# Two state-space stages: their preparation moved into the stages before them, and every fourth unit's product given to GpSimd

## What is computed

```python
x = einsum('ed,bld->bel', in_proj_w, ctx)              # ctx (4, 256, 128), not the residual
u = silu(depthwise_conv4(x) + conv_b)
x_dbl = einsum('ke,bel->bkl', x_proj_w, u)             # 8 + 16 + 16 rows: dt_lo, Bm, Cm
delta = softplus(einsum('er,brl->bel', dt_proj_w, dt_lo) + dt_proj_b)
def step(state, xs):                                   # over the 256 tokens, 16 states a channel
    dA = exp(d_t[..., None] * A)
    state = state * dA + (d_t * u_t)[..., None] * B_t[:, None, :]
    y_t = einsum('ben,bn->be', state, C_t)
    ...
y = (ys + D[None, :, None] * u) * silu(z)              # z is the layernorm of the residual
```

## Time and profile before

| | |
|---|---|
| time, median of 3 runs | 1869.97 us (1865.51 to 1870.55) |
| the profiled execution, its own time | 1874.38 us |
| its span, first to last instruction | 1872.6 us |
| busy: PE, DVE, ACT, POOL | 60%, 59%, 25%, 32% of the span |
| mean granted clock of PE, share of 2.4 GHz | 0.806 |
| mean DMA rate | 99 GB/s |

### The profile page before, as it was taken

How to read it: one execution, slowest core, us unless ns; L and a number is a source line. 1 busy time by engine, 2 the same in 40 slices (tenths; PEclk the granted TensorE clock), 3 DMA queues, 4 the chain that set the end, 5 groups by cost and what they waited for, 6 DMA issues and landing times. The chain is left out here.

```text
span 1872.6 us, 21908 instructions
## 1 busy us (share of the span) xinstructions
PE 1121.4 (60%) x5649; PEld 707.2 (38%) x5650; DVE 1106.5 (59%) x1869; ACT 476.3 (25%) x883; POOL 604.8 (32%) x646
## 2 busy tenths in 40 slices
PE   5315556995085961552697802698847558846870
PEld 2201134774044730211454602576624124435750
DVE  5759974444354537998876695411448537562463
ACT  2143311221012533330211100333212226602320
POOL 0016623444631103661200073034232212214555
PEclk8669976998587975996798856799978559968995
DMA  6023347993307011421000001224410550078843
GB/s 217 1 93 135 134 127 232 304 310 92 98 23 113 4 58 59 157 90 67 0 1 1 1 11 34 75 99 130 125 42 12 68 57 4 3 230 269 254 134 101
DMA packets 135045, 185.54 MB, mean 99 GB/s; under 512 B 34656, under 2 KB 98802, under 8 KB 134332
## 3 DMA queue, kind: packets, MB, share of 16 engines
q1 hardware_dynamic: 99084, 131.89, 25.0%
q0 software_dynamic: 12608, 31.26, 6.0%
q10 hardware_dynamic: 23280, 21.50, 3.5%
HBM read 140.97 MB, written 30.74 MB: 92 GB/s over the span
## 5 line engine op out<-in xcount | busy, mean ns | idle before, releaser
L172 PE MATMUL psum<-w_ident,h 128*128 128x128 f32 x144 | 32.0, 414 | 145.8 <-DVE h L150 145.8
L1542 DVE TENSOR_REDUCE l3x_neg<-psum 128x2 f32<-128x512 f32 x128 | 81.0, 684 | 61.6 <-PE psum L1414 61.5
L462 PE MATMUL psum<-l0s_conv_out,w_ident 128*128 128x512 f32 x128 | 65.0, 632 | 83.5 <-DVE l0s_conv_out L559 83.5
L462 PE MATMUL psum<-l1s_conv_out,w_ident 128*128 128x512 f32 x128 | 65.5, 637 | 81.4 <-DVE l1s_conv_out L559 81.4
L160 POOL TENSOR_SCALAR rstd<-moments 128x4 f32<-128x4 f32 x24 | 6.5, 270 | 320.0 <-DVE moments L143 320.0
L1517 ACT ACTIVATE l3x_work<-psum 128x512 f32<-128x512 f32 x128 | 72.3, 599 | 89.6 <-PE psum L1436 89.3
L428 POOL TENSOR_TENSOR l0s_xpad<-l0s_du,l0s_bc 128x1024 f32<-128x1024 f32 x32 | 75.2, 2353 | 32.6 <-DVE psum L555 32.4
L428 POOL TENSOR_TENSOR l1s_xpad<-l1s_du,l1s_bc 128x1024 f32<-128x1024 f32 x32 | 75.2, 2353 | 32.5 <-DVE psum L555 32.4
L184 ACT ACTIVATE hT<-psum 128x512 f32<-128x512 f32 x40 | 21.7, 595 | 250.0 <-PE psum L172 210.1
L172 PEld LDWEIGHTS psum<-w_ident,h 128*128 128x128 f32 x144 | 28.0, 218 | 150.4 <-DVE h L150 139.6
L985 PE MATMUL psum<-l0f_w_in,l0f_xT 128*128 (+1 forms) x224 | 78.0, 472 | 3.3 <-ACT l0f_xT L1031 3.3
(11 more groups left out here) (643 smaller groups left out, 3179.5 us busy)
## 6 DMA issues: line engine op xcount, KB each, us to landing
l0f_w_in<-in_l0f_w_in SPq DMA_DIRECT2D x56, 352.0 KB, 8.3
l0s_bc<-l0s_scratch SPq DMA_DIRECT2D x16, 1024.0 KB, 5.2
l1s_bc<-l1s_scratch SPq DMA_DIRECT2D x16, 1024.0 KB, 5.3
l3f_w_in<-in_l3f_w_in SPq DMA_DIRECT2D x64, 192.0 KB, 4.1
...
```

The source lines that it names most:

```text
L172: ins = nc.tensor.transpose(m.psum[:, at:at + P], m.h[:, t, k * P:(k + 1) * P], m.ident[:])
L462: ins = nc.tensor.matmul(m.pair(2 + c)[:, cols], lhsT=m.ident[:], rhs=rhs[:, cols], start=start, stop=stop, skip_group_check=True)
L1542: ins = nc.vector.tensor_reduce(self.neg[k % 2][:, :, hl], bank[:, 0:self.keys].rearrange("p (q k) -> p q k", q=self.maxima), AX_X, ALU.ma ...
```

## The change

The function `state_space` becomes a class with methods that other stages call. Layer 0's preparation runs within stage 0, layer 1's at the end of stage 2, in buffers borrowed there; what is kept until the scan is `u`, `delta`, for layer 0 also the first slot of `bc`, and for layer 1 two chunks that lie in the space of the weights `l3x_` and `l3a_`, which are now loaded in stage 5 (by SP, behind that stage's own three loads). The scan stage itself loads the slots at its start, forms `du` on DVE, then the layernorm, and runs the units. In every fourth unit (`handed`: u % 4 == 3, always chunk 1) DVE scans into an SBUF tile `handed_state` and POOL multiplies it by C into `handed_read`; the waits count accordingly. `convolve`, `project_in`, `project_x`, `project_dt`, `take_in`, `take_conv`, `take_x`, `take_dt` and `store_rows` hold the same instructions as L538/L540, L439, L446, L453, L492, L496, L501, L505 to L513 and L393/L397 before; `soften` is L582 and `softplus_tail`. In stage 0 the two attention chunks get exp and relu tiles of their own.

```diff
@@ -273,22 +278,27 @@
...
+    e = [[m.sb(f"l0_exp{c}{i}", [P, T]) for i in range(2)] for c in range(KD)]
+    relu = [m.sb(f"l0_relu{c}", [P, 2, T]) for c in range(KD)]
+    r = [[relu[c][:, i, :] for i in range(2)] for c in range(KD)]
     sums = [m.sb(f"l0_sum{i}", [P, T]) for i in range(2)]
     att = m.sb("l0_att", [P, KD, T])
-    phi_in = m.sem("l0_phi_in")
     chunk_done = m.sem("l0_chunk_done")
+    flat = lambda x: x[:].rearrange("p t d -> p (t d)").rearrange("p (k t) -> p k t", k=KD)
+    ssm.prepare(xpad=m.sb("l0s_xpad", [P, KD, B, D_CONV - 1 + S])[:], conv=m.sb("l0s_conv_out", [P, KD, T])[:], t_sq=flat(m.h),
+                relu=relu[0][:], xdbl=m.hT[0:X_DBL, 0, :])
...
+            m.load_weights(sp, [g for g in reversed(m.w_loaded) if g not in FIRST_WEIGHTS + LATE_WEIGHTS])
+            ssm.store_rows(sp)
...
+            ssm.project_in(pe, (m.pair(2), m.pair(3)))
             norm_tensor(m, pe, n)
             m.wait_weights(pe, "l0_attn")
+            pe.wait_ge(ssm.x_out, KD)
             for c in range(KD):
                 for i, x in enumerate("qkv"):
                     project(m, pe, jobs, x + str(c), wcols(w, KD * i + c), feature_rhs(m.hT), KD,
                             turn=j if c + i == 0 else None)
+            pe.wait_ge(jobs.emptied["vector"], 1)
+            ssm.project_x(pe, m.pair(0, X_DBL))
+            pe.wait_ge(jobs.emptied["scalar"], 2 * KD)
+            ssm.project_dt(pe, (m.pair(1), m.pair(2)))
             pe.wait_ge(chunk_done, KD)
+            pe.wait_ge(ssm.dt_taken, KD)
...
+            ssm.take_in(act, (m.pair(2), m.pair(3)))
             norm_scalar(m, act, j)
             for c in range(KD):
                 for i, x in enumerate("qk"):
                     name = x + str(c)
                     jobs.wait_filled(act, name)
-                    if c:
-                        act.wait_ge(chunk_done, c)
-                    nc.scalar.activation(e[i][:], jobs.pair(name), ACT.Exp).then_inc(phi_in, 1)
-                    nc.scalar.activation(r[i][:], jobs.pair(name), ACT.Relu).then_inc(jobs.empty(name), 1)
+                    nc.scalar.activation(e[c][i][:], jobs.pair(name), ACT.Exp)
+                    nc.scalar.activation(r[c][i], jobs.pair(name), ACT.Relu).then_inc(jobs.empty(name), 1)
+            ssm.take_conv(act)
+            ssm.take_x(act, m.pair(0, X_DBL))
+            act.wait_ge(chunk_done, 1)
+            ssm.take_dt(act, (m.pair(1), m.pair(2)))
...
+                ssm.convolve(dve, c)
+            for c in range(KD):
                 dve.wait_ge(jobs.emptied["scalar"], 2 * c + 2)
...
                 nc.vector.tensor_tensor(att[:, c, :], sums[0][:], sums[1][:], ALU.mult).then_inc(chunk_done, 1)
+            ssm.soften(dve, 0)
             add_tokens(m, dve, jobs, ("out0", "out1"), scale=16 ** -0.5)
...
+            ssm.soften(dve, 1)
...
+    def soften(self, dve, c):
+        nc, o = self.m.nc, self.m.dve_order
+        dve.wait_ge(self.act_dt, c + 1)
+        e, q = self.delta[:, c, :], self.t_sq[:, c, :]
+        o.link(dve, nc.vector.tensor_tensor(e, e, q, ALU.mult))
+        softplus_tail(dve, nc.vector, o, e, q, self.conv[:, c, :], self.relu[:, c, :], e)
...
+        handed = lambda u: u % 4 == 3
+        reads = [sum(not handed(v) for v in range(u)) for u in range(UNITS + 1)]
+        by_pool = [sum(handed(v) for v in range(u)) for u in range(UNITS + 1)]
+        handed_state, handed_read = m.sb(g + "handed_state", [P, T]), m.sb(g + "handed_read", [P, T])
...
+                norm_gpsimd(m, pool, n)
+                pool.wait_ge(du_ready, 1)
+                def read_for(i, q0, u):
+                    pool.wait_ge(summed, q0 + (u + KD + 1 - 4))
+                    nc.gpsimd.tensor_tensor(handed_read[:], handed_state[:], bc[u // KD][:, 1, :], ALU.mult).then_inc(
+                        handed_ready, 1)
+                def group(i, q0, first):
+                    for s in range(SLOTS):
+                        pool.wait_ge(bc_in[s], (i + 1) * 16)
                         for c in range(KD):
...
+                            u = s * KD + c
+                            pool.wait_ge(scanned, q0 + u + 1)
+                            nc.gpsimd.tensor_tensor(drive[c], du[:, c, :], bc[s][:, 0, :],
+                                                    ALU.mult).then_inc(drive_ready, 1)
+                            if u >= KD and handed(u - KD):
+                                read_for(i, q0, u - KD)
+                            if not first and u < KD and handed(u - KD + UNITS):
+                                read_for(i, q0 - UNITS, u - KD + UNITS)
+                group(0, 0, True)
+                with pool.Fori(1, GROUPS) as i:
+                    group(i, i * UNITS, False)
+                pool.wait_ge(scanned, GROUPS * UNITS + KD)
+                read_for(GROUPS - 1, (GROUPS - 1) * UNITS, UNITS - 1)
...
+                            if handed(u):
+                                pe.wait_ge(handed_ready, i * by_pool[UNITS] + (by_pool[u] + 2))
+                            else:
+                                pe.wait_ge(read_ready, i * reads[UNITS] + (reads[u] + 1 + KD))
...
+                            if handed((unit - KD) % UNITS):
+                                act.wait_ge(scanned, i * UNITS + (unit + 1))
+                            else:
+                                before = reads[unit + 1 - KD] if unit >= KD else reads[unit + 1 - KD + UNITS] - reads[UNITS]
+                                act.wait_ge(read_ready, i * reads[UNITS] + (before + KD))
...
+                dve.sem_inc(handed_ready, 1)
+                for c in range(KD):
+                    o.mark(nc.vector.tensor_tensor(du[:, c, :], delta[:, c, :], u[:, c, :], ALU.mult))
+                o.wait(dve)
+                for c in range(KD):
+                    first = delta[:, c, :].rearrange("p (b s) -> p b s", s=S)[:, :, 0:1]
+                    o.mark(nc.vector.memset(first, 1e25))
+                o.wait(dve)
+                dve.sem_inc(du_ready, 1)
+                norm_vector(m, dve, n)
+                def unit(i, s, c):
+                    u, q = s * KD + c, i * UNITS + (s * KD + c)
+                    dve.wait_ge(decay_ready, q + 1)
+                    dve.wait_ge(drive_ready, q + 1)
+                    if handed(u):
+                        dve.wait_ge(handed_ready, i * by_pool[UNITS] + (by_pool[u] + 1))
+                    out = handed_state[:] if handed(u) else state[c]
+                    nc.vector.tensor_tensor_scan(out, decay[c], drive[c], 0.0, ALU.mult, ALU.add).then_inc(scanned, 1)
+                    if not handed(u):
+                        dve.wait_ge(scanned, q + 1 + KD)
+                        dve.wait_ge(summed, q + 1)
+                        nc.vector.tensor_tensor(read[c], state[c], bc[s][:, 1, :], ALU.mult).then_inc(read_ready, 1)
...
+SOFTENED = (0, 20, 32)
...
             by_steps(pe, groups, step, 3)
+            if ssm is not None:
+                ssm.project_in(pe, (m.pair(0), m.pair(1)))
+                ssm.project_x(pe, m.pair(2, X_DBL))
+                ssm.project_dt(pe, (m.pair(0), m.pair(1)))
...
             by_steps(act, groups, step, 4)
+            if ssm is not None:
+                ssm.take_in(act, (m.pair(0), m.pair(1)))
+                ssm.take_conv(act)
+                ssm.take_x(act, m.pair(2, X_DBL))
+                ssm.take_dt(act, (m.pair(0), m.pair(1)))
...
             for q in range(K * TILES):
+                if ssm is not None and q == SOFTENED[0]:
+                    for c in range(KD):
+                        ssm.convolve(dve, c)
+                if ssm is not None and q in SOFTENED[1:]:
+                    ssm.soften(dve, SOFTENED.index(q) - 1)
...
+            m.load_weights(sp, LATE_WEIGHTS)
...
-FIRST_WEIGHTS = ("consts", "l0_attn")
+FIRST_WEIGHTS = ("consts", "l0s_", "l0_attn")
+LATE_WEIGHTS = ("l3x_", "l3a_")
...
-            lambda n, j: linear_attention(m, n, j),
-            lambda n, j: state_space(m, 0, n),
-            lambda n, j: experts(m, n, j, "l0f_", routed=16, top=6, rows=88, chunks=2, ahead=16),
+            lambda n, j: linear_attention(m, n, j, ssm[0]),
+            lambda n, j: ssm[0].scan(n),
+            lambda n, j: experts(m, n, j, "l0f_", routed=16, top=6, rows=88, chunks=2, ahead=16, ssm=ssm[1]),
             lambda n, j: softmax_attention(m, n, j, "l1a_", heads=16, causal=True),
-            lambda n, j: state_space(m, 1, n),
+            lambda n, j: ssm[1].scan(n),
```

More of the change, by code:

```diff
@@ L457, in _ @@
-            pe.wait_ge(skip_ready, KD)
-            def add(c, rhs, start, stop):
-                for half in range(2):
-                    cols = slice(half * HALF, (half + 1) * HALF)
-                    ins = nc.tensor.matmul(m.pair(2 + c)[:, cols], lhsT=m.ident[:], rhs=rhs[:, cols], start=start,
-                                           stop=stop, skip_group_check=True)
-                return ins
-            for c in range(KD):
-                add(c, skip[:, c, :], True, False)
```

(12 more changed lines are left out.)

424 lines of the change are left out of this document (224 added, 200 removed).

## The result

The changed kernel took 1809.7 us in the median (1806.88 to 1818.93, 4 runs) against 1870.26 (1865.51 to 1871.55); the ratio is 0.9689 (95% interval 0.965 to 0.9729). The forecast was 1802, range 1778 to 1817. The profiled execution took 1811.52, its span is 1809.7: 62.9 less than before, where the forecast's sum was 67.8.

What follows compares the result with a forecast made beforehand. The prediction took DVE to bound the scan loop and a scan-free chain of engines the preparation. Its terms, -40.2 - 56.6 + 8 + 21 = -67.8, gave 1802 us against the median, range 1778 to 1817.

Steps and rivals of the forecast that it cites:

- The moved preparation: Preparation moved into earlier stages: first drive 40.2 us earlier in layer 0 and 56.6 earlier in layer 1.
- 0.7 for POOL's first product beside DVE's norm products: Scan stage's start: POOL's first product beside DVE's two-input norm products adds 0.7 us before the first drive.
- Handing gains nothing: Scan loop: a chain through the late handed add returns DVE's saved 1.2 as waiting; four units take 13.73 us.
- 1.3 a cycle by the clock: Scan loop: PE's clock falls in most idle gaps, lengthening handed adds; 1.3 us a cycle, eight cycles a layer.
- the term for the last unit, +0.4: End of each scan loop: the last unit's handed read costs the small gain from handing; 0 or +0.4 us.
- The tail's +8: End of stage 2, hosting layer 1's preparation: later additions and slower gathers cost 8 us, bounds +5 and +15.
- The price of 0.3 to 0.6 for each gather beside a two-input product: End of stage 2: DVE's two-input products slow gathers by 0.3 to 0.6 each, ending the last up to 10 later.
- Rival B: Scan loop: PE's clock stays at 2.4 GHz through the gaps, scan term 0; total 1781 us, chance 18%.
- D: Scan loop: handed read works as intended, DVE bounds at 12.66 us a cycle; total 1762, chance 5%.
- E: Scan loop: POOL's product and DVE's exclude each other, 24.5 us a cycle for 13.7; total about 1952, chance 2%.
- C: Gathers starved in stage 2's tail (+15 and above) or every add at 1.2 GHz (+14 a layer); 1809 to 1817, 13%.
- A: The forecast itself: in the scan loop handing gains nothing and costs by the clock; 1794 to 1811 us, chance 60%.

Runs made afterwards that it cites:

- e6: The changed kernel with GpSimd's first product waiting until the layernorm's products on VectorE are done; 1816.92 us in one run, scan stages 144.3 and 145.5.
- e5: The changed kernel with four matmuls of zeros keeping TensorE busy before it waits for each handed product; 1790.55 us in one run.
- e2: The changed kernel with handed adds two units later, reads waiting only for the last add out of their own buffer; 1791.46 us, ratio 0.9564.
- f4: The changed kernel with tensor_scalars heading convolutions and softplus polynomials made scalar_tensor_tensor, changing the preparation's values; 1826.65 us in one run.

## Why the prediction was right, and where its sizes were off

**The moved preparation** was right in mechanism and nearly in size: first drive 39.75 earlier for 40.2, in layer 1 (64.91 before, from 646.16 to 653.90, 7.74, after) 57.2 for 56.6; stage 0 took one more than forecast, since its first chunk came at 27.22 and not 25.8. No loaded slot was late.

**"0.7 for POOL's first product beside DVE's norm products" was mis-sized, and put on the wrong engine.** I looked for a later product on POOL. It was DVE's norm products that were held, behind them stands the first scan, and it cost 2.95 a layer. These products are tensor_scalars with one tensor as input, not the two-input products that the prediction calls them. Its own price row already showed more than 0.7: 3.25 for 1.22 is 2.0 lost, the same 2.0 as here for each product of GpSimd that is met. e6 takes half of the 2.95 back.

**"Handing gains nothing"** was right, by the chain named: with the clock kept up (e5) a cycle takes 13.77, for 13.73 forecast, and e2 takes the chain away and brings 12.89, where the prediction put DVE's own work at 12.66. The forecast's sum is loose: its seven durations alone are 13.70, which leaves no room for the handoffs that it names. Nor do three adds stand back to back ahead of the gap; the last one before it follows an idle time of 1.42. **"1.3 a cycle by the clock"** was right in cause (e5) and short in size: the clock fell in every gap and not in most, and cost 15.38 - 13.77 = 1.61. Against the cycle of before that is 15.38 - 13.84 = 1.54, over seven cycles 10.8; and the term for the last unit, +0.4, was 2.7, since behind the last handed scan both the handed read (2.34) and an add at 1.2 GHz (3.53) lie bare. Together 13.4 and 13.2 a layer instead of 10.5 (which is itself a little short: eight times 1.3 and 0.4 are 10.8).

**The tail's +8** was +3.9, of which the gathers were 3.95 longer, DVE's end 0.8 later still and the part ahead of the first gather, where the code is the same, 0.8 shorter. DVE's side had been forecast at +5. The price of 0.3 to 0.6 for each gather beside a two-input product was the wrong step: such products left gathers at 0.95 to 1.02. The Trainium skill ("SBUF — State Buffer", "Who interferes with whom") has it that descriptor generation is held by the two-port modes and tensor_tensor has none; I let one row of 1.30 speak against it. f4 agrees for the three gathers behind tensor_scalars, which are gone with them. The fourth long one and something smaller (60.4 for 58.8, single gathers of 1.21 and 1.31) stay unexplained by any run here.

The sum: +11.45 for the two loops and the first scans (13.35 + 13.2 + 2 x 2.95 - 2 x 10.5), -4.1 for the tail, +0.45 and -0.6 for the first drives and -2.5 in the untouched stages take the forecast's -67.8 to -63.1; measured were -62.9. That the total came so near is in part luck: the tail's overestimate and the untouched stages hide 6.6 of the 11.45. Rival B (clock stays) falls with the window at 0.50, D with DVE's idle of 3.01, E with scans that stay at 2.28. C falls by 3.9 in the tail, and by the adds ahead of each gap, which still take 1.98 (at 159.39); its time of 1809 to 1817 doesn't tell it from A, whose own terms reach 1814 and not the 1811 stated.
